# The last layer normalisation of a decoder layer, in pieces of two tiles and with its steps dealt out anew among VectorE, ScalarE and GpSimd

## The chip, the core and the metric

The kernel runs on one core of a Trainium2 chip. Its time is device time in microseconds (us), and the times below are medians of runs of the whole kernel. A profiled execution gives the rows: each names an engine (PE is TensorE's matrix multiply and PEld its weight load, DVE is VectorE, ACT is ScalarE, POOL is GpSimd, SP is SyncE, which here only issues transfers), a line of the kernel, and what was written from what.

## The reference

A decoder layer on x of 2 x 1024 tokens with 256 features, in float32: self attention, cross attention to 77 rows, and a mixture of 8 experts of which each token takes two. Each of the three ends in a residual sum and a layer normalisation. The change is in the third.

```
def _layernorm(x, g, b):
    m = x.mean(-1, keepdims=True)
    v = ((x - m) ** 2).mean(-1, keepdims=True)
    return (x - m) / jnp.sqrt(v + 1e-05) * g + b
...
x = _layernorm(x + _attn(x, x, x, sa_wq, ..., True), ln1_g, ln1_b)
x = _layernorm(x + _attn(x, encoder_output, encoder_output, ca_wq, ..., False), ln2_g, ln2_b)
x = _layernorm(x + _moe(x, router_w, router_b, e_w1, e_b1, e_w2, e_b2), ln3_g, ln3_b)
```

## The kernel before

The 2048 tokens stand in 16 tiles of 128 tokens, one token in a partition: `res` (called residual in the rows) is 128 x 16 x 256 in SBUF. Each engine has one instruction stream, written out by hand, and the streams meet through semaphores (`wait_ge` waits, `then_inc` counts up when the instruction is done). Attention and routing follow a plan, a string of letters that is the same for all engines. Behind it comes a loop over tiles of tokens sorted by expert: TensorE multiplies, ScalarE applies the Gelu (L1123), VectorE adds the bias and the weight (L1345, L1347), and GpSimd adds the finished rows into the table `sums_d` (sums_scratch) in HBM by indirect transfers (L1821).

When the last of these has landed, the third normalisation begins, and nothing else runs from there to the end. It goes over 16 tiles in pieces of `PIECE = 4`:

- SyncE issues the loads of all four pieces from `sums_d` into `res`, 512 KB each (L2085). Then it waits for each finished piece and stores it (L2088), and at last for the stores.
- VectorE takes mean and variance of each tile, `bn_stats` (L1310) and `bn_aggr` (L1312), of which the second waits for the first. After piece n it multiplies the tiles of piece n-1 by the gain row (`gain`, L1352), which waits for ScalarE's result.
- GpSimd makes 1/sqrt(variance + eps) of a piece by a guess and three Newton steps (`normal_scale`, L1792 to L1809): 17 small instructions, in a chain of which each waits for the one ahead. Afterwards it adds the bias row to the tiles of piece n-1 (`shifted`, L1828).
- ScalarE makes x * rstd - mean * rstd of each tile (L1302) as soon as GpSimd has the two columns of that piece.

In GpSimd's stream `normal_scale` of piece n stands ahead of the four adds of piece n-1. `normal_scale` serves the first two normalisations too; lines L1475 and L1478 are theirs on VectorE for half of the tiles, where one `scalar_tensor_tensor` subtracts the mean and multiplies by the gain row, and another scales and adds.

Of the kernel before, what the change touches and what calls it, by code (L numbers as in the profile page):

```python
# [59 lines left out]
PIECE = 4  # L60
# [301 lines left out]
def build(nc, x, ctx_in, par, wts, router_w, w1, b1, w2, b2, out):  # L362
# [3 lines left out]
    with stack:  # L366
# [6 lines left out]
        def sems(name, n):  # L373
            return [sem(f"{name}{i}") for i in range(n)]
# [20 lines left out]
        rstd = sb("rstd", [P, NT])  # L395
        newton = sb("newton", [P, 4, QT])
# [217 lines left out]
        for it in find("proj"):  # L614
# [3 lines left out]
        x_in = sems("x_in", B * NG)  # L618
# [21 lines left out]
        maxima_ok, biased, stats_ok, sdev_ok, scaled = (  # L640
            sem("maxima_split"), sem("out_bias_added"), sem("stats_ok"), sem("sdev_ok"), sem("scaled"))
        scaled_last, sums_stats_ok, tops_ok = sem("sums_scaled"), sem("sums_stats_ok"), sem("tops_ok")
        centred, gained, normal_v, normal_g = sem("centred"), sem("gained"), sem("normal_v"), sem("normal_g")
        chosen, hot_ok, counted, routed = sem("chosen"), sem("hot_ok"), sem("counted"), sem("routed")
        logit_sum, logits_taken = sem("logits_summed"), sem("logits_taken")
        exps_in, exps_ok, diff_ok, second_ok = sem("exps_in"), sem("exps_ok"), sem("diff_ok"), sem("second_exp")
        totals_ok, rows_placed, ej_ok = sem("totals_ok"), sem("rows_placed"), sem("tile_experts_ok")
# [13 lines left out]
        sums_in, stored = sems("sums_in", NT // PIECE), sem("out_stored")  # L661
# [70 lines left out]
        def normal_in(cross, b, t):  # L732

            return (normal_v if b else normal_g, apply_n[cross, b, t])

# [36 lines left out]
        def tensor(pe):  # L772
# [47 lines left out]
            for it in plan:  # L820
# [5 lines left out]
                if it.kind in ("xt", "r_turn"):  # L826
                    if it.kind == "r_turn" or it.cross:
                        e.wait_ge(*normal_in(it.kind == "r_turn", it.b, it.t))
                    else:
                        e.wait_ge(x_in[it.b * NG + it.t // QT], 16)  # L830
# [275 lines left out]
        def scalar(act_e):  # L1106
# [191 lines left out]

            for n in range(NT // PIECE):
                act_e.wait_ge(scaled_last, n + 1)  # L1300
                for t in range(n * PIECE, (n + 1) * PIECE):
                    act_e.activation(res[:, t, :], res[:, t, :], ACT.Identity, scale=rstd[:, t:t + 1],  # L1302
                                     bias=shift[:, t:t + 1]).then_inc(centred, 1)


        def vector(dve):
# [41 lines left out]

            def gain(t, row):
                e.wait_ge(centred, N_APPLY + t + 1)  # L1350
                e.wait_ge(param_in, (NPARAM + 1) * 16)
                dve.tensor_tensor(res[:, t, :], res[:, t, :], param[:, row, :], ALU.mult).then_inc(gained, 1)  # L1352
# [415 lines left out]

            for n in range(NT // PIECE):
                e.wait_ge(sums_in[n], 16)  # L1770
                for t in range(n * PIECE, (n + 1) * PIECE):
                    statistics(t, sums_stats_ok)
                for m in ([n - 1] if n else []) + ([n] if n == NT // PIECE - 1 else []):
                    for t in range(m * PIECE, (m + 1) * PIECE):
                        gain(t, G3)


        def gpsimd(pool):
# [45 lines left out]

            def shifted(t, row):
                e.wait_ge(gained, t + 1)
                e.wait_ge(param_in, (NPARAM + 1) * 16)
                pool.tensor_tensor(res[:, t, :], res[:, t, :], param[:, row, :], ALU.add).then_inc(normal_g, 1)  # L1828
# [129 lines left out]
            for n in range(NT // PIECE + 1):  # L1958
                if n < NT // PIECE:
                    e.wait_ge(sums_stats_ok, (n + 1) * PIECE)  # L1960
                    normal_scale(n * PIECE, scaled_last)
                for t in range((n - 1) * PIECE, n * PIECE) if n else ():
                    shifted(t, B3N)


        def sync(sp):
            e = Waiting(sp)
            for b in range(B):
                for u in range(NG):
                    t0 = b * TB + u * QT  # L1970
                    sp.dma_start(res[:, t0:t0 + QT, :], x[b, u * QG:(u + 1) * QG].rearrange(
                        "(t p) n -> p t n", p=P)).then_inc(x_in[b * NG + u], 16)
# [149 lines left out]
```

## Time and profile before

| | |
|---|---|
| median of 3 runs (825.37 to 833.92) | 826.38 us |
| profiled execution, its own time | 823.76 us |
| its span, first to last instruction | 821.9 us |
| PE, DVE, ACT, POOL busy, share of the span | 87%, 50%, 46%, 34% |
| issue of the first load of the last normalisation (L2085) | at 775.82 us |
| first bn_stats of the last normalisation | at 779.90 us |
| issue of the last store (L2088) | at 815.27 us |

The span starts at 0, so the last three lines are places in it. The first four engines' shares are means over the whole span; the last 46 us have another mix, which the windows and the timeline show. Idle time of an engine that does not set the end costs nothing.

### The profile page before, as it was taken

How to read it: one execution, taken by the hardware profiler on the slowest of the kernel's cores; microseconds unless marked ns; L12 is line 12 of the kernel's file. 1: busy time of each engine (PE TensorE's matmuls, PEld its weight loads, DVE VectorE, ACT ScalarE, POOL GpSimd, SP SyncE). 2: the span in 40 equal slices, each digit the busy share in tenths (PEclk: the TensorE clock that was granted, in tenths of full speed). 3: DMA queues.
4: the chain of work that ended last, by engine and by line, in shares of the span. 5: the costliest groups of instructions: out<-in, count | busy, mean ns of one | idle time of the engine just before them, and what ended most of it. 6: DMA issues, size and time to landing. Idle time of an engine off the chain costs nothing.

```text
span 821.9 us, 14648 instructions
## 1 busy us (share of the span) xinstructions
PE 717.3 (87%) x5227; PEld 491.9 (60%) x5227; DVE 407.2 (50%) x964; ACT 375.0 (46%) x764; POOL 277.4 (34%) x502
## 2 busy tenths in 40 slices
PE   6789999999999999999987699993999999999400
PEld 4434444545555555555535578983999999999300
DVE  5668776757757777655785451662111011111153
ACT  3224555565665766777544444330433333333121
POOL 8140300321352323315622152314133333232276
PEclk9969999999999999999998899996999999999755
DMA  9960430452127013113147639877699999999422
GB/s 288 299 148 1 130 104 4 119 154 80 43 76 205 15 42 117 45 51 91 41 160 272 196 109 271 241 239 261 207 322 328 324 328 324 313 341 274 121 72 77
DMA packets 98528, 140.42 MB, mean 171 GB/s; under 512 B 11647, under 2 KB 85605, under 8 KB 95973
## 3 DMA queue, kind: packets, MB, share of 16 engines
q1 hardware_dynamic: 78453, 110.08, 42.3%
q10 hardware_dynamic: 12896, 19.92, 7.4%
q0 software_dynamic: 7104, 9.45, 5.8%
q8 instruction: 43, 0.70, 0.4%
q14 instruction: 32, 0.26, 0.1%
HBM read 108.55 MB, written 30.88 MB: 170 GB/s over the span
## 4 chain that ended last, share of the span: by engine, by line
PE 51%; DMA 31%; POOL 5%; issue 5%; DVE 2%; ACT 2%; SPq 2%; ACTq 1%; POOLq 0%; DVEq 0%
DMA sums_scratch<-arena,scatter_rows 22%; PE out_acc L946 10%; PE score_pair L923 8%; PE work L893 8%; PE work L867 4%; PE work L810 4%; PE work L816 3%; PE work L970 3%; DMA arena<-parts_scratch 3%; DMA parts_scratch<-arena_more 2%; PE score_pair L926 2%; PE work L954 2%; POOL residual L1828 1%; PE work L896 1%; PE work L879 1%
## 5 line engine op out<-in xcount | busy, mean ns | idle before, releaser
L1420 DVE TENSOR_REDUCE neg_part_max<-work 128x1 f32<-128x512 f32 (+4 forms) x368 | 213.3, 625 | 88.2 <-PE work L893 43.5
L1190 ACT ACTIVATE arena<-score_pair 128x1024 f32<-128x1024 f32 (+2 forms) x224 | 178.7, 839 | 92.6 <-PE score_pair L926 60.7
L893 PE MATMUL work<-arena 96*128 96x77 bf16 (+4 forms) x640 | 122.2, 284 | 14.1 <-DMA arena<-parts_scratch 6.4
L923 PE MATMUL score_pair<-arena 99*128 99x512 bf16 (+2 forms) x448 | 113.0, 335 | 4.3 <-DMA arena<-negmax_scratch 3.0
L1821 POOL DMA_INDIRECT sums_scratch<-arena,scatter_rows x36 | 56.7, 1574 | 177.5 <-DMA sums_scratch<-arena,scatter_rows 127.9
L946 PE MATMUL out_acc<-arena 128*32 128x512 f32 (+4 forms) x896 | 104.5, 517 | 5.6 <-ACT arena L1190 5.0
L816 PE MATMUL score_pair<-arena 128*128 128x256 f32 x432 | 97.5, 379 | 0.0
L893 PEld LDWEIGHTS work<-arena 96*128 96x128 bf16 x640 | 49.5, 100 | 78.8 <-issue 39.7
L1345 DVE TENSOR_TENSOR arena<-score_pair,arena 128x256 f32<-128x256 f32 x27 | 11.5, 424 | 170.6 <-PE score_pair L816 161.1
L810 PE MATMUL work<-arena 128*128 128x128 f32 x720 | 86.2, 278 | 1.0 <-ACT arena L1123 0.5
L816 PEld LDWEIGHTS score_pair<-arena 128*128 128x128 f32 x432 | 80.1, 190 | 9.8
L810 PEld LDWEIGHTS work<-arena 128*128 128x128 f32 x720 | 83.7, 194 | 1.6 <-ACT arena L1123 0.6
L1123 ACT ACTIVATE arena<-work,expert_b_cols 128x128 f32<-128x128 f32 x180 | 51.2, 370 | 66.3 <-issue 36.1
L923 PEld LDWEIGHTS score_pair<-arena 99*128 99x128 bf16 (+1 forms) x448 | 41.7, 101 | 52.8 <-issue 24.1
L810 PE MATMUL score_pair<-arena 128*128 128x128 f32 x432 | 50.5, 275 | 0.0
L926 PE MATMUL score_pair<-identb,mask_qk 128*128 128x128 bf16 x256 | 49.8, 219 | 0.0
L810 PEld LDWEIGHTS score_pair<-arena 128*128 128x128 f32 x432 | 49.4, 192 | 0.1
L896 PE MATMUL work<-mask_qk,identb 128*128 128x128 bf16 x256 | 49.2, 222 | 0.0
L1872 POOL TENSOR_TENSOR arena<-arena,arena_more 128x512 f32<-128x512 f32 (+1 forms) x18 | 19.1, 1063 | 88.8 <-ACT arena L1153 88.8
L1123 ACT ACTIVATE arena<-score_pair,expert_b_cols 128x128 f32<-128x128 f32 x108 | 31.0, 370 | 37.4 <-PE score_pair L810 29.4
L867 PE MATMUL work<-arena_more,arena 128*128 128x512 f32 x96 | 47.4, 624 | 0.1
L946 PEld LDWEIGHTS out_acc<-arena 128*32 128x32 f32 (+1 forms) x896 | 19.5, 108 | 36.5 <-issue 27.9
(238 smaller groups left out, 906.2 us busy)
## 6 DMA issues: line engine op xcount, KB each, us to landing
arena<-in_L_xattn_e_w SPq DMA_DIRECT2D x54, 1024.0 KB, 7.8
arena<-parts_scratch SPq DMA_DIRECT2D x24, 768.0 KB, 6.4
arena<-in_L_xattn_e_w ACTq DMA_DIRECT2D x18, 1024.0 KB, 6.2
parts_scratch<-arena_more SPq DMA_DIRECT2D x24, 384.0 KB, 3.3
parts_scratch<-arena_more SPq DMA_DIRECT2D x24, 256.0 KB, 3.4
parts_scratch<-arena_more SPq DMA_DIRECT2D x24, 128.0 KB, 3.6
residual<-in_x SPq DMA_DIRECT2D x4, 512.0 KB, 8.1
tokens_scratch<-residual SPq DMA_DIRECT2D x2, 1024.0 KB, 6.0
```

Source lines behind the costliest of these rows:

```text
L810: m = pe.matmul(to[:, q * P:(q + 1) * P], w1_ring[j % RING1][:, c, f * P:(f + 1) * P], slot_xT[j % 2][:, c, :], start=(c == 0), stop=(c == ...
L816: m = pe.matmul(to, act[j % 2][:, c, :], w2_ring[j % RING2][:, c, :], start=(c == 0), stop=(c == FC - 1))
L867: m = pe.matmul(bank[:, 0:it.w], weights[:, c, st.hh * P:(st.hh + 1) * P], src, start=(c == 0), stop=(c == KC - 1))
L893: m = pe.matmul(bank[:, j * it.w:(j + 1) * it.w], qa[st.half(it.g)][0:R_S, h, n0:n0 + P], k, start=True, stop=not it.last)
L896: m = pe.matmul(bank[:, (j + 1) * it.w - P:(j + 1) * it.w], identb[:, :], mask_qk[:, :], start=False, stop=True)
L923: m = pe.matmul(st2[pair][0:rows, j, 0:w], k, qa[st.half(it.g)][0:R_M, h, skip:QG], start=True, stop=not diagonal)
L926: m = pe.matmul(st2[pair][:, j, 0:P], mask_qk[:, :], identb[:, :], start=False, stop=True)
L946: m = pe.matmul(o_ps[c * VW:(c + 1) * VW, skip:QG], v, pt[buf][0:rows, j, 0:QG - skip], start=first, stop=last)
L1123: m = act_e.activation(act[j % 2][:, c, :], bank[:, q * P:(q + 1) * P], ACT.Gelu, bias=b1_col[:, bass.ds(ex * FC + c, 1)])
L1190: act_e.activation(pt[buf][0:rows, :, 0:w], st2[pair][0:rows, :, 0:w], ACT.Exp, scale=float(HD) ** -0.5).then_inc(pair_taken[pair], 1)
L1420: dve.tensor_reduce(pm[:, it.at, it.t, it.h0:it.h0 + it.nh], bank[:, 0:it.nh * it.w].rearrange("p (j k) -> p j k", j=it.nh), AX.X, ALU.max ...
L1821: pool.indirect_dma_start(sums_d[0:S] if j < NFIRST else sums_d, bass.IndirectOffsetOnAxis(ap=rows_out[:, j:j + 1], axis=0), slot_y[j % RI ...
```

## The change

Pieces are of two tiles: eight loads and eight stores of 256 KB. VectorE takes the statistics of the two tiles, first both `bn_stats`, then both `bn_aggr`. With the mean it then makes (x - mean) * gain in one `scalar_tensor_tensor` per tile, and a `reciprocal` of the two roots that ScalarE has made meanwhile. ScalarE takes the square root of the variances of piece n, and scales the tiles of piece n-1. GpSimd adds the bias row to each tile and does nothing else. One square root of a constant stands ahead of the loop on ScalarE. The loads' semaphores are shared with those of x at the program's start. The first two normalisations are as they were.

```diff
-PIECE = 4
+PIECE = 2
...
+        root = sb("deviation", [P, NT + 1])
...
@@ scalar @@
-            for n in range(NT // PIECE):
-                act_e.wait_ge(scaled_last, n + 1)
-                for t in range(n * PIECE, (n + 1) * PIECE):
-                    act_e.activation(res[:, t, :], res[:, t, :], ACT.Identity, scale=rstd[:, t:t + 1],
-                                     bias=shift[:, t:t + 1]).then_inc(centred, 1)
+            act_e.activation(root[:, NT:], epsc[:, :], ACT.Sqrt)
+            for n in range(NT // PIECE + 1):
+                if n < NT // PIECE:
+                    tiles = slice(n * PIECE, (n + 1) * PIECE)
+                    act_e.wait_ge(sums_stats_ok, (n + 1) * PIECE)
+                    act_e.activation(root[:, tiles], mv[:, tiles, 1], ACT.Sqrt, bias=epsc[:, :]).then_inc(root_ok, 1)
+                for t in range((n - 1) * PIECE, n * PIECE) if n else ():
+                    act_e.wait_ge(inverted, n)
+                    act_e.activation(res[:, t, :], res[:, t, :], ACT.Identity, scale=rstd[:, t:t + 1]).then_inc(sums_scaled, 1)
@@ vector @@
-            for n in range(NT // PIECE):
-                e.wait_ge(sums_in[n], 16)
-                for t in range(n * PIECE, (n + 1) * PIECE):
-                    statistics(t, sums_stats_ok)
-                for m in ([n - 1] if n else []) + ([n] if n == NT // PIECE - 1 else []):
-                    for t in range(m * PIECE, (m + 1) * PIECE):
-                        gain(t, G3)
+            e.wait_ge(param_in, (NPARAM + 1) * 16)
+            for n in range(NT // PIECE):
+                tiles = range(n * PIECE, (n + 1) * PIECE)
+                e.wait_ge(*sums_in(n))
+                for t in tiles:
+                    own.inc(dve.bn_stats(stat[:, t % 2, :], res[:, t, :]))
+                e.wait_ge(vstep, own.n)
+                for t in tiles:
+                    dve.bn_aggr(mv[:, t, :], stat[:, t % 2, :]).then_inc(sums_stats_ok, 1)
+                e.wait_ge(sums_stats_ok, (n + 1) * PIECE)
+                for t in tiles:
+                    m = dve.scalar_tensor_tensor(res[:, t, :], res[:, t, :], mv[:, t, 0:1], param[:, G3, :],
+                                                 ALU.subtract, ALU.mult)
+                e.wait_ge(root_ok, n + 1)
+
+                dve.reciprocal(rstd[:, n * PIECE:(n + 1) * PIECE], root[:, n * PIECE:(n + 1) * PIECE]).then_inc(inverted, 1)
@@ gpsimd @@
-            for n in range(NT // PIECE + 1):
-                if n < NT // PIECE:
-                    e.wait_ge(sums_stats_ok, (n + 1) * PIECE)
-                    normal_scale(n * PIECE, scaled_last)
-                for t in range((n - 1) * PIECE, n * PIECE) if n else ():
-                    shifted(t, B3N)
+            e.wait_ge(param_in, (NPARAM + 1) * 16)
+            for t in range(NT):
+                e.wait_ge(sums_scaled, t + 1)
+                pool.tensor_tensor(res[:, t, :], res[:, t, :], param[:, B3N, :], ALU.add).then_inc(normal_g, 1)
@@ sync @@
-                sp.dma_start(res[:, n * PIECE:(n + 1) * PIECE, :], rows_of(sums_d, n * PIECE)).then_inc(sums_in[n], 16)
+                sp.dma_start(res[:, n * PIECE:(n + 1) * PIECE, :], rows_of(sums_d, n * PIECE)).then_inc(sums_in(n)[0], 16)
```

The change moves instructions on three engines, all behind the expert loop. VectorE at the end of piece 1 before: the statistics go tile by tile, and the four gains of the piece ahead stand between two pieces.

```order
L1310 BN_STATS stat<-residual 128x6
L1312 BN_AGGR mean_var<-stat 128x2
L1352 TENSOR_TENSOR residual<-residual,param_rows 128x256 x4
L1310 BN_STATS stat<-residual 128x6
L1312 BN_AGGR mean_var<-stat 128x2
```

VectorE after, a whole piece and the start of the next (deviation is `root`, rstd its reciprocal):

```order
L1780 BN_STATS stat<-residual 128x6 x2
L1783 BN_AGGR mean_var<-stat 128x2 x2
L1786 SCALAR_TENSOR_TENSOR residual<-residual,mean_var,param_rows 128x256 x2
L1790 RECIPROCAL rstd<-deviation 128x2
L1780 BN_STATS stat<-residual 128x6 x2
```

The pass over the full tile that VectorE adds is now right behind the statistics of the same piece, and one small instruction closes the piece.

ScalarE before, from the last Gelu of the expert loop to its end:

```order
L1123 ISA
L1123 ACTIVATE arena<-work,expert_b_cols 128x128
L1293 UNCONDITIONAL_BRANCH
L1295 UNCONDITIONAL_BRANCH
L1302 ACTIVATE residual<-residual,minus_mean_scaled,rstd 128x256 x16
L366 UNCONDITIONAL_BRANCH
```

ScalarE after, from the same place on (L1129 is the Gelu, L1306 the root of the constant, L1311 the roots of a piece, L1314 the scaling):

```order
L1129 ACTIVATE arena<-work,expert_b_cols 128x128
L1299 UNCONDITIONAL_BRANCH
L1301 UNCONDITIONAL_BRANCH
L1306 ACT_TABLE_LOAD
L1306 ACTIVATE deviation<-eps 128x1
L1311 ACTIVATE deviation<-mean_var,eps 128x2 x2
L1314 ACTIVATE residual<-residual,rstd 128x256 x2
L1311 ACTIVATE deviation<-mean_var,eps 128x2
L1314 ACTIVATE residual<-residual,rstd 128x256 x2
```

One table load came in, behind the Gelus, and the roots of piece n+1 stand ahead of the scalings of piece n.

GpSimd before, its last instructions, which are the end of the Newton chain of the last piece and eight adds:

```order
L1803 TENSOR_SCALAR newton<-newton 128x4
L1805 TENSOR_TENSOR rstd<-newton,rstd 128x4
L1807 TENSOR_TENSOR newton<-mean_var,rstd 128x4
L1809 TENSOR_SCALAR minus_mean_scaled<-newton 128x4
L1828 TENSOR_TENSOR residual<-residual,param_rows 128x256 x8
L366 UNCONDITIONAL_BRANCH
```

GpSimd after, from the last indirect transfer (L1836) on:

```order
L1964 COMPARE_AND_BRANCH
L1836 DMA sums_scratch<-arena,scatter_rows 2176x256
L1964 UNCONDITIONAL_BRANCH
L1971 TENSOR_TENSOR residual<-residual,param_rows 128x256 x16
L366 UNCONDITIONAL_BRANCH
```

The 17 small instructions of each of the four pieces are gone, and the 16 adds are left.

## Rows read from the trace of the kernel before

**Rows 1.** The chain that ended last, 779.9 to 815.3 us, its shares by line.

```profile
by line: POOL residual L1828 33.0%; issue 14.3%; POOL newton L1803 8.5%; POOL newton L1801 7.7%; POOL newton L1799 7.6%; POOL rstd L1805 7.1%; DVE stat L1310 4.0%; POOL rstd L1795 3.0%; POOL newton L1792 3.0%; POOL newton L1794 2.7%; POOL m
```

**Rows 2.** Timeline of the last normalisation: start, length (us), instruction [idle before].

```profile
775.82 2.03 SPq L2085 DMA_DIRECT2D residual<-sums_scratch  x4
779.90 0.43 DVE L1310 BATCH_NORM_STATS2 stat<-residual 128x6 f32<-128x256 f32 x1 [9.67 <-DMA residual<-sums_scratch]
780.36 0.18 DVE L1312 BATCH_NORM_AGGREGATE mean_var<-stat 128x2 f32<-128x6 f32 x1
780.46 0.39 DVE L1310 BATCH_NORM_STATS2 stat<-residual 128x6 f32<-128x256 f32 x1
...
787.09 2.07 ACT L1302 ACTIVATE residual<-residual,minus_mean_scaled,rstd 128x256 f32<-128x256 f32 x4 [23.53 <-POOL minus_mean_scaled L1809]
787.72 1.90 DVE L1352 TENSOR_TENSOR residual<-residual,param_rows 128x256 f32<-128x256 f32 x4 [3.48 <-ACT residual L1302]
...
792.83 3.13 POOL L1828 TENSOR_TENSOR residual<-residual,param_rows 128x256 f32<-128x256 f32 x4
793.53 3.05 DVE L1352 TENSOR_TENSOR residual<-residual,param_rows 128x256 f32<-128x256 f32 x4 [1.78 <-ACT residual L1302]
...
800.93 3.13 POOL L1828 TENSOR_TENSOR residual<-residual,param_rows 128x256 f32<-128x256 f32 x4
...
815.27 0.37 SPq L2088 DMA_DIRECT2D out<-residual  x1
```

**Rows 3.** Single lines, ns of one instruction as min/median/max, first and last start.

```profile
L1828 POOL TENSOR_TENSOR residual<-residual,param_rows x16: 717/812/907, 792.8 to 814.5; 128x256 f32<-128x256 f32 x16
L1352 DVE TENSOR_TENSOR residual<-residual,param_rows x16: 412/938/986, 787.7 to 812.4; 128x256 f32<-128x256 f32 x16
L1302 ACT ACTIVATE residual<-residual,minus_mean_scaled,rstd x16: 585/586/600, 787.1 to 810.6; 128x256 f32<-128x256 f32 x16
L1475 DVE SCALAR_TENSOR_TENSOR residual<-residual,mean_var,param_rows x16: 474/479/594, 344.1 to 528.4; 128x256 f32<-128x256 f32 x16
L1226 ACT ACTIVATE combine<-weight_tmp x2: 208/208/208, 444.4 to 559.1; 128x8 f32<-128x8 f32 x2
```

**Rows 4.** Transfers from 775 us on: size, median issue to landing; loads' landing by min/median/max.

```profile
residual<-sums_scratch SPq DMA_DIRECT2D x4, 512.0 KB, 5.6
out<-residual SPq DMA_DIRECT2D x4, 512.0 KB, 2.9
DMA to landing us min/median/max: 4.1/5.6/6.9
```

**Rows 5.** Windows from the first load's issue: engines' busy time, last number GB/s.

```profile
775.80:778.80 3.00, 0.00 (x0) 0.00 (x0) 0.00 (x0) 0.00 (x0) 0.00 (x0) 0.50 0.47 129
775.80:779.90 4.10, 0.00 (x0) 0.00 (x0) 0.00 (x1) 0.00 (x0) 0.00 (x0) 0.50 0.63 195
```

**Rows 6.** Timeline of VectorE in the first normalisation.

```profile
344.74 0.49 DVE L1478 SCALAR_TENSOR_TENSOR residual<-residual,rstd,param_rows 128x256 f32<-128x256 f32 x1
345.14 0.48 DVE L1475 SCALAR_TENSOR_TENSOR residual<-residual,mean_var,param_rows 128x256 f32<-128x256 f32 x1
```

**Rows 7.** Timeline at 413 us: statistics on VectorE beside an add on GpSimd.

```profile
413.28 0.73 POOL L1907 TENSOR_TENSOR residual<-residual,param_rows 128x256 f32<-128x256 f32 x1
...
413.58 0.43 DVE L1310 BATCH_NORM_STATS2 stat<-residual 128x6 f32<-128x256 f32 x1
```

**Rows 8.** Groups of VectorE by form: count, busy us and mean ns, idle before.

```profile
L1406 DVE SCALAR_TENSOR_TENSOR arena<-work,bias_columns,arena_more 128x512 f32<-128x512 f32 x8 | 6.0, 750 | 8.9 <-ACT arena_more L1148 8.9
...
L1406 DVE SCALAR_TENSOR_TENSOR arena<-work,bias_columns,arena_more 128x77 f32<-128x77 f32 x2 | 0.6, 299 | 3.3 <-ACT arena_more L1148 3.3
...
L1686 DVE RECIPROCAL prob_recip<-prob_recip 128x8 f32<-128x8 f32 x2 | 0.4, 203 | 0.1
```

**Rows 9.** Timeline of ScalarE at a table load in the routing.

```profile
550.64 1.28 ACT L1220 ACT_TABLE_LOAD   x1
551.93 0.26 ACT L1220 ACTIVATE arena_more<-arena_more 128x64 f32<-128x64 f32 x1
```

More of the change, by code:

```diff
@@ L615, in build @@
             first_of[it.n] = sum(z.st.in_a_hurry for z in find("proj")[:it.n]) + 1
-        x_in = sems("x_in", B * NG)
+        res_in = sems("residual_in", NT // PIECE)
         w_self_in = sems("w_self_in", 4)
@@ L639, in build @@
         vstep, astep, gstep = sem("vector_step"), sem("scalar_step"), sem("gpsimd_step")
[L640 to L644, printed above, removed]
+        maxima_ok, biased, stats_ok, scaled = (
+            sem("maxima_split"), sem("out_bias_added"), sem("stats_ok"), sem("scaled"))
+        sums_scaled, sums_stats_ok, tops_ok = sem("sums_scaled"), sem("sums_stats_ok"), sem("tops_ok")
+        root_ok, inverted = sem("root_ok"), sem("roots_inverted")
+        centred, normal_v, normal_g = sem("centred"), sem("normal_v"), sem("normal_g")
+        hot_ok = sem("hot_ok")
         logit_sum, logits_taken = sem("logits_summed"), sem("logits_taken")
         exps_in, exps_ok, diff_ok, second_ok = sem("exps_in"), sem("exps_ok"), sem("diff_ok"), sem("second_exp")
-        totals_ok, rows_placed, ej_ok = sem("totals_ok"), sem("rows_placed"), sem("tile_experts_ok")
+        rows_placed, ej_ok = sem("rows_placed"), sem("tile_experts_ok")
         rows_ok, kinds_ok, out_rows_ok = sem("rows_ok"), sem("kinds_ok"), sem("out_rows_ok")
@@ L660, in build @@
         y_ok = sem("y_ok")
-        sums_in, stored = sems("sums_in", NT // PIECE), sem("out_stored")
+        stored = sem("out_stored")
         up_banks = work + [st2[1][:, 0, :], st2[1][:, 1, :], o_ps[:, :]]
@@ L734, in normal_in, with sums_in @@
             return (normal_v if b else normal_g, apply_n[cross, b, t])
+        def sums_in(n):
+            return res_in[n], 16 * (2 if n < B * NG else 1)
         def kuse_in(st):
@@ L829, in tensor @@
                     else:
-                        e.wait_ge(x_in[it.b * NG + it.t // QT], 16)
+                        e.wait_ge(res_in[it.b * NG + it.t // QT], 16)
                     e.wait_ge(ident_ok, 1)
@@ L1347, in weighted @@
                 dve.tensor_scalar(y, y, w_slot[:, j:j + 1], None, ALU.mult).then_inc(y_ok, 1)
[L1349 to L1352, printed above, removed]
             dve.memset(ident[:, :], 0.0).then_inc(zeroed, 1)
@@ L1823, in add_up @@
                     compute_op=ALU.add).then_inc(slot_y_out(j)[0], 16)
[L1825 to L1828, printed above, removed]
             e.wait_ge(zeroed, 1)
@@ L1971, in sync @@
                     sp.dma_start(res[:, t0:t0 + QT, :], x[b, u * QG:(u + 1) * QG].rearrange(
-                        "(t p) n -> p t n", p=P)).then_inc(x_in[b * NG + u], 16)
+                        "(t p) n -> p t n", p=P)).then_inc(res_in[b * NG + u], 16)
             for i in range(4):
```

## The prediction

> **What bounds the kernel now.** I read the page's chain first. Most of it is attention and the expert loop, which the change doesn't touch; what matters here is that the last normalisation runs alone, so that every microsecond saved in it is one of the span. It starts with the loads at 775.82 us and ends with the span at 821.9. Its parts: 4.1 us until the first load has landed [rows 2], 35.3 us from the first bn_stats at 779.9 to the end of the last add, and 6.7 us behind that, for the last store (issue at 815.27, 2.9 us to landing [rows 2, 4]) and the program's end, 3.7 us.
>
> For the 35.3 us I read the chain by line [rows 1]. The adds of L1828 and the small instructions of the Newton chain fill nearly all of it, GpSimd's two jobs one after the other. The timeline says how fast it goes: the adds of one piece of four tiles start at 792.83, those of the next at 800.93 [rows 2]. So a piece costs 8.1 us, 3.1 for four adds and the rest for the 17 chained instructions. ScalarE stood idle for 23.5 us ahead of its first scaling [rows 2], VectorE waits for ScalarE. GpSimd is the bound of this stage by a wide margin.
>
> **The change part by part.** I lay a new timetable, piece of two tiles by piece.
>
> Removed from GpSimd: 4 x 17 small instructions. That leaves 16 adds. One alone takes 0.72 us and the next starts 0.68 after it, so its floor is 10.9 us, far below the rest of this sum. The adds only have to keep up.
>
> VectorE, per piece. An instruction that doesn't wait for the one ahead starts 0.08 us before that one's end (aggr at 780.36 for 0.18, the next stats at 780.46 [rows 2]); one that waits starts 0.03 to 0.04 after it (stats 779.90 for 0.43, aggr at 780.36). With 0.39 for bn_stats and 0.18 for bn_aggr: first stats 0.31, second 0.43 with the wait behind it, first aggr 0.10, second 0.22 with the wait. The new full pass has its own row in the first normalisation, same operation, same shape, same kind of scalar: 0.479 us at the median [rows 3], and 0.40 from one start to the next when nothing is waited for (344.74 to 345.14 [rows 6]). Two of them 0.80. The reciprocal is 0.20 us, from a row of 8 columns where here there are 2 [rows 8], 0.12 until the next start. Sum: 0.31 + 0.43 + 0.10 + 0.22 + 0.80 + 0.12 = 1.98 us a piece.
>
> ScalarE, per piece: a small activation at 0.21 [rows 3] and two scalings of 0.59 that start about 0.5 apart (four in 2.07 [rows 2]), 1.15 us of issue in all. That is under VectorE's 1.98. The roots are asked for when the statistics are done and are ready 0.25 later; VectorE wants them 0.8 later, behind its two passes. So the root costs nothing as long as those passes cover it. In ScalarE's queue the root of piece n+1 stands ahead of the scaling of piece n, so the scaling waits for the statistics of the next piece: a lag of about 1 us, paid by nobody until the last piece, where no root stands in front.
>
> The added wait of VectorE is the one on the roots, with the next piece's statistics queued behind it. The added waits of GpSimd queue nothing but adds.
>
> The table load. ScalarE's last Gelu is over 23.5 us before 787.09, at 763.6 [rows 2]; the load and the root of the constant stand right behind it, 12 us ahead of the first load's issue. A load takes 1.28 us, and the next activation starts 1.29 after the load's start [rows 9]. Hidden, and without that cover it would cost 1.3. The build has one such row behind the Gelus, so scaling needs no other table.
>
> SyncE's queue gets eight issues at about 0.5 us each instead of four (2.03 us for four [rows 2]). The eighth load leaves some 2 us later than the fourth did. VectorE wants piece 7 only 14 us after piece 0, so that is hidden. The first piece, half as large, is where I expect a small gain. The 512 KB piece was there at 779.9, when 195 GB/s x 4.1 us = 800 KB had been moved in all, since pieces behind it share the engines. At the same share 262 KB are there when 400 KB have moved, which the trace had about 778.8 (129 x 3.0 = 387 [rows 5]). Bounds 778.8 and 779.9; I take 779.0.
>
> The last store is half as large. 512 KB took 2.9 us to land; loads streamed 512 KB in about 1.4 us at full rate (800 - 387 KB in 1.1 us), so half of that less gives 2.2. Bounds 1.9 and 2.9.
>
> Now the sum. First statistics 779.0; those of piece 0 done 1.0 later (0.31 + 0.43 + 0.10 + 0.18): 780.0. Those of piece 7 come 7 x 1.98 = 13.9 later: 793.9. Behind them on ScalarE: root 0.24, scalings of piece 6 until 1.24, those of piece 7 ending at 1.8 and 2.3. GpSimd adds piece 6 from 0.9 to 2.2 and piece 7 from 2.2 to 3.6: 797.5. Store 2.2, program's end 3.7: span 803.4, against 821.9. That is 18.5 us less, 805.3 for the profiled execution. It stands 2.6 us under the median of 826.38; taken off the median the 18.5 give **807.9**, and I say 808.0.
>
> **Contention.** What the sum leaves out is that VectorE's passes with two inputs in SBUF and GpSimd's adds hold each other up. L1352 takes 0.41 alone and 0.94 beside an add, and the adds go from 0.72 to 0.91 [rows 3]; four gains take 1.90 us alone and 3.05 beside adds, which then take 3.13 for four [rows 2]. Statistics are free of it: bn_stats wholly inside an add took 0.43 as ever [rows 7]. In my timetable adds of piece n-1 run from 0.9 to 2.2 us behind piece n's statistics, and VectorE's passes from 0.0 to 0.85 and from 2.0 on. So the adds lie mostly beside statistics and touch a pass by 0.1 or 0.2 us. This is luck of phase. I leave it at nothing and put the bad phase among the rivals.
>
> A rule speaks against the new pass. The row shows 0.479 us for `scalar_tensor_tensor` on two float32 tiles in SBUF against 0.41 for `tensor_tensor` on such tiles [rows 3]. The Trainium skill, Vector Engine (DVE) Microarchitecture Reference, section 7 (Points that are easy to get wrong), says that a `scalar_tensor_tensor` with two SBUF sources other than bf16 runs at half throughput. By that rule the passes would be longer and the forecast 4.1 us later, which is the second rival; the trace of before disagrees, in 16 instructions of that very form.
>
> **Rivals.**
>
> Lockstep. Passes and adds meet every time. The phase isn't fixed: a pass that is held up ends later, which pulls the next piece's adds along. Then each of the two passes costs what a gain cost between adds, 0.88 from start to start ((3.05 - 0.41) / 3 [rows 2, 3]), and a piece 1.98 + 2 x 0.48 = 2.94 us. 7 x 2.94 = 20.6 in place of 13.9: 6.7 more, 814.6. For it: the rows of L1352. Against it: GpSimd is idle for a third of each piece, and the timetable puts that third beside the passes. The Trainium skill, GPSIMD Engine Reference, section 1 (Specifications), says that its SBUF interfaces are shared with VectorE, with contention from VectorE instructions that have two SBUF inputs; the rows above agree.
>
> The pass at half rate. An element costs 1.04 ns in this operation, (750 - 299) / (512 - 77) [rows 8]; twice that for 256 elements adds 0.27 us a pass, 0.53 a piece, 3.7 over seven pieces, and 0.4 at the end, where the last reciprocal would now come later than ScalarE's queue allows: 812.1. Against it: the 0.479 above.
>
> The change doesn't do what it says: ScalarE changes table for every root and back. 2 x 1.29 more in a piece [rows 9] makes ScalarE the bound, 2.6 + 1.15 + 0.1 = 3.85 a piece; 780.0 + 8 x 3.85 + 0.7 + 2.2 + 3.7 = 817.4, 4.5 less than before: 821.9, within 1%. Against it: the build has one load.
>
> Slower. Each of the eight loads pays its whole time from issue to landing behind the one ahead, as if they went one by one: 5.6 us each [rows 4], last at 775.8 + 44.8 = 820.6, then 1.0 + 3.6 + 2.2 + 3.7 for the rest: span 831.1, 835.6 on the median. It decides from 4.45 us a load. Against it: the four loads before were all in within 8.4 us, though each took 4.1 to 6.9.
>
> **How the numbers follow.** The timetable as laid, 0.75. Lockstep 0.12, half rate 0.04, table changes 0.03, one-by-one loads 0.02; 0.04 for what I don't see. The main case alone has the bounds 778.8 and 1.9 below (0.5 less) and 779.9, 2.9 and a held-up first pass of 0.2 a piece above (0.9 + 0.7 + 1.4 = 3.0 more), so 807.4 to 811. Medians of three wander by about a microsecond (825.37 and 826.38 among the three of before), and my step times could be off by a tenth a piece to either side, which is why the range begins at 805.5. Above it goes to 812.5, which takes in half rate and the milder half of lockstep. What a measurement can tell from no change is about 1%, 8 us. Faster by more than that: all but tables, loads and part of the unseen, 0.93. Within 1%: 0.05. Slower: 0.02.
>
> **What would show it.** In the trace of the changed kernel: a table load near 764 us and none later; the first bn_stats at about 779.0; starts of the first bn_stats of neighbouring pieces 2.0 apart, with VectorE busy throughout and idle for no root; the new pass at 0.48, and at 0.6 or more where an add crosses it; adds 0.68 apart in pairs with gaps between pairs; eight stores 2 us apart; the last add ending near 797.5. A distance of 2.5 or 2.9 speaks for a rival. I would be wrong if an instruction stream stalls where I laid none: ScalarE late with a root, since that sits in one queue with the scalings, or a pass caught in every piece.

## The result and the profile after

The changed kernel took 806.52 us at the median of 4 runs (801.18 to 807.22), the kernel before 827.04 (825.37 to 833.92): a ratio of 0.9745, with a 95% interval of 0.9709 to 0.978. The forecast was 808.0, from 805.5 to 812.5. The same kernel run again later, beside the kernel before, gave 805.98 against 824.4, a ratio of 0.9791 (0.9763 to 0.9819).

The profiled execution took 807.22 us with a span of 805.4. Its first load went out at 777.63 us, 1.8 later than in the profile of before; that head wanders by a few microseconds from one execution to the next (777.63 and 774.12 in the two profiles of the changed kernel), and no instruction was moved in it. So I compare the last stretch, from the issue of the first load to the end of the span: 46.1 us before, 27.8 after, 18.3 less. The forecast for it was 18.5. The second profile of the changed kernel gives 27.8 again.

The chain of the stretch from 777 us on, its shares by line (lines of the changed kernel: L1786 is VectorE's pass, L1780 and L1783 the statistics, L1971 the adds):

```profile
by line: DVE residual L1786 22.0%; DVE stat L1780 18.6%; DMA residual<-sums_scratch 9.5%; POOL residual L1971 7.2%; DVE mean_var L1783 7.2%; issue 3.2%; POOLq L366 2.3%; DVE rstd L1790 1.8%; ACT residual L1314 1.4%; ACT deviation L1311 1.0%
```

In [rows 1] nearly all was GpSimd's. Now VectorE has the chain, and GpSimd only its end. The timeline, for the first load, pieces 0 to 2, and the last piece (start, length, instruction, idle before):

```profile
777.63 3.96 SPq L2093 DMA_DIRECT2D residual<-sums_scratch  x8
780.40 0.75 DVE L1780 BATCH_NORM_STATS2 stat<-residual 128x6 f32<-128x256 f32 x2 [8.49 <-DMA residual<-sums_scratch]
781.18 0.25 DVE L1783 BATCH_NORM_AGGREGATE mean_var<-stat 128x2 f32<-128x6 f32 x2
781.47 0.30 ACT L1311 ACTIVATE deviation<-mean_var,eps 128x2 f32<-128x2 f32 x1 [13.55 <-DVE mean_var L1783]
781.47 0.88 DVE L1786 SCALAR_TENSOR_TENSOR residual<-residual,mean_var,param_rows 128x256 f32<-128x256 f32 x2
782.27 0.16 DVE L1790 RECIPROCAL rstd<-deviation 128x2 f32<-128x2 f32 x1
782.34 0.73 DVE L1780 BATCH_NORM_STATS2 stat<-residual 128x6 f32<-128x256 f32 x2
...
784.24 1.40 POOL L1971 TENSOR_TENSOR residual<-residual,param_rows 128x256 f32<-128x256 f32 x2 [9.43 <-ACT residual L1314]
784.26 0.73 DVE L1780 BATCH_NORM_STATS2 stat<-residual 128x6 f32<-128x256 f32 x2
785.03 0.25 DVE L1783 BATCH_NORM_AGGREGATE mean_var<-stat 128x2 f32<-128x6 f32 x2
...
785.32 1.00 DVE L1786 SCALAR_TENSOR_TENSOR residual<-residual,mean_var,param_rows 128x256 f32<-128x256 f32 x2
...
785.67 13.42 SPq L2096 DMA_DIRECT2D out<-residual  x8
786.09 1.49 POOL L1971 TENSOR_TENSOR residual<-residual,param_rows 128x256 f32<-128x256 f32 x2 [0.45 <-ACT residual L1314]
...
792.16 0.73 DVE L1780 BATCH_NORM_STATS2 stat<-residual 128x6 f32<-128x256 f32 x2
...
794.11 0.73 DVE L1780 BATCH_NORM_STATS2 stat<-residual 128x6 f32<-128x256 f32 x2
...
795.15 0.30 ACT L1311 ACTIVATE deviation<-mean_var,eps 128x2 f32<-128x2 f32 x1 [0.86 <-DVE mean_var L1783]
795.15 0.90 DVE L1786 SCALAR_TENSOR_TENSOR residual<-residual,mean_var,param_rows 128x256 f32<-128x256 f32 x2
795.36 1.72 ACT L1314 ACTIVATE residual<-residual,rstd 128x256 f32<-128x256 f32 x4
795.92 2.77 POOL L1971 TENSOR_TENSOR residual<-residual,param_rows 128x256 f32<-128x256 f32 x4 [0.55 <-ACT residual L1314]
```

Read against [rows 2]: pieces of two tiles now start 1.92 to 1.95 us apart (780.40, 782.34, 784.26, and near the end 792.16, 794.11), where four tiles took 8.1. Nothing is left between VectorE's steps but gaps of 0.02 to 0.04 us. The last add ends at 795.92 + 2.77 = 798.69, and the span 6.7 us later, as before. The single lines, against [rows 3] (ns as min/median/max):

```profile
L1786 DVE SCALAR_TENSOR_TENSOR residual<-residual,mean_var,param_rows x16: 472/482/607, 781.5 to 795.6; 128x256 f32<-128x256 f32 x16
...
L1971 POOL TENSOR_TENSOR residual<-residual,param_rows x16: 717/722/811, 784.2 to 798.0; 128x256 f32<-128x256 f32 x16
...
L1314 ACT ACTIVATE residual<-residual,rstd x16: 491/492/507, 783.6 to 796.6; 128x256 f32<-128x256 f32 x16
```

The new pass takes what its row of the first normalisation said. The adds are back at 0.72 but for one, and the scaling is 0.09 us shorter without its bias column. The transfers, against [rows 4]:

```profile
residual<-sums_scratch SPq DMA_DIRECT2D x8, 256.0 KB, 4.4
out<-residual SPq DMA_DIRECT2D x8, 256.0 KB, 2.1
```

### The profile page after: what moved, and what is told of

Its sections match the earlier page's. It is cut to its first block, busy times and chain, and to the rows that moved or that the text cites. A ratio compares the mean times of both kernels' runs of the same rounds, so it can differ in the third digit from the quotient of the medians.

```text
span 805.4 us, 14606 instructions
## 1 busy us (share of the span) xinstructions
PE 720.3 (89%) x5227; PEld 496.8 (62%) x5227; DVE 404.0 (50%) x972; ACT 376.5 (47%) x774; POOL 260.7 (32%) x434
## 4 chain that ended last, share of the span: by engine, by line
PE 54%; DMA 29%; DVE 5%; issue 5%; ACT 2%; POOL 2%; ACTq 1%; SPq 1%; POOLq 0%; DVEq 0%
DMA sums_scratch<-arena,scatter_rows 22%; PE out_acc L952 10%; PE score_pair L929 8%; PE work L899 8%; PE work L873 5%; PE work L816 4%; DMA arena<-parts_scratch 4%; PE work L822 3%; PE work L976 3%; PE work L885 2%; DVE neg_part_max L1426 2%; PE score_pair L932 2%; PE work L960 2%; PE work L902 2%; DMA parts_scratch<-arena_more 1%
## 5 line engine op out<-in xcount | busy, mean ns | idle before, releaser
L1836 POOL DMA_INDIRECT sums_scratch<-arena,scatter_rows x36 | 56.7, 1574 | 179.4 <-DMA sums_scratch<-arena,scatter_rows 127.4
L816 PE MATMUL work<-arena 128*128 128x128 f32 x720 | 89.8, 285 | 0.7 <-ACT arena L1129 0.5
L816 PEld LDWEIGHTS work<-arena 128*128 128x128 f32 x720 | 87.3, 201 | 1.4 <-ACT arena L1129 0.6
L1129 ACT ACTIVATE arena<-work,expert_b_cols 128x128 f32<-128x128 f32 x180 | 51.1, 369 | 69.2 <-issue 37.7
L1129 ACT ACTIVATE arena<-score_pair,expert_b_cols 128x128 f32<-128x128 f32 x108 | 30.9, 369 | 37.4 <-PE score_pair L816 29.4
```

The source lines that it names most:

```text
L816: m = pe.matmul(to[:, q * P:(q + 1) * P], w1_ring[j % RING1][:, c, f * P:(f + 1) * P], slot_xT[j % 2][:, c, :], start=(c == 0), stop=(c == ...
L1129: m = act_e.activation(act[j % 2][:, c, :], bank[:, q * P:(q + 1) * P], ACT.Gelu, bias=b1_col[:, bass.ds(ex * FC + c, 1)])
L1836: pool.indirect_dma_start(sums_d[0:S] if j < NFIRST else sums_d, bass.IndirectOffsetOnAxis(ap=rows_out[:, j:j + 1], axis=0), slot_y[j % RI ...
```

## The experiments

All are read by the last stretch, from the first load's issue to the end of the span, and by the distance between pieces in it. The head varies more than most of these effects, while the stretch repeats within 0.1 us: 27.8 in both profiles of the changed kernel, 31.2 and 31.1 in the two forms with pieces of four. Whole times stand where a kernel was timed in several runs.

**Small pieces with the old dealing out.** The kernel before with pieces of two, with the loads' semaphores shared as in the changed kernel:

```diff
-PIECE = 4
+PIECE = 2
...
-            def normal_scale(t0, done):
+            def normal_scale(t0, done, n=QT):
...
-                    normal_scale(n * PIECE, scaled_last)
+                    normal_scale(n * PIECE, scaled_last, PIECE)
```

Expected: 

> The kernel before with pieces of two tiles and nothing else: the Newton chain stays on GpSimd, now on two columns and eight times instead of four. Theory A (the gain of the change comes from taking the chain off GpSimd): a chain costs about 4.9 us whatever its width, since it is 17 small instructions that wait for each other, so 8 x 4.9 + 16 adds in 12.4 us = 52 us in place of 33; the first load lands 1.3 us sooner and the first statistics are done 1.1 us sooner, so the span is about 16.5 us longer than before, some 843 us. Theory B (the gain comes from the smaller pieces, which overlap better): shorter than before by a good part of the 18 us.

Measured: 840.0 us against 823.44 of before, ratio 1.0187 (1.0148 to 1.0227), and 61.9 us for the last stretch. GpSimd's timeline, from the first instruction of a chain to that of the next:

```profile
797.72 1.41 POOL L1831 TENSOR_TENSOR residual<-residual,param_rows 128x256 f32<-128x256 f32 x2
799.21 0.27 POOL L1795 TENSOR_SCALAR newton<-mean_var 128x2 f32<-128x2 f32 x1
804.01 1.41 POOL L1831 TENSOR_TENSOR residual<-residual,param_rows 128x256 f32<-128x256 f32 x2
```

A chain on two columns takes 4.8 us, from 799.21 to 804.01, and one on four columns 5.0 (8.1 less 3.1 for the adds [rows 2]). Theory A holds. Small pieces alone, without the new dealing out, cost 15.8 us.

**The new dealing out with pieces of four.** The changed kernel with

```diff
-PIECE = 2
+PIECE = 4
...
-        stat = sb("stat", [P, 2, 6])
+        stat = sb("stat", [P, 4, 6])
...
-                    own.inc(dve.bn_stats(stat[:, t % 2, :], res[:, t, :]))
+                    own.inc(dve.bn_stats(stat[:, t % 4, :], res[:, t, :]))
...
-                    dve.bn_aggr(mv[:, t, :], stat[:, t % 2, :]).then_inc(sums_stats_ok, 1)
+                    dve.bn_aggr(mv[:, t, :], stat[:, t % 4, :]).then_inc(sums_stats_ok, 1)
```

Expected: 

> The changed kernel with pieces of four tiles. Theory A (the dealing out of the steps is what pays): from the first load's issue to the end about 2.3 us more than the 27.8 us of the changed kernel, 1.3 of it because 512 KB land 1.3 us later than 256 KB and 1.0 because the last piece's four adds trail behind VectorE. Theory B (piece size is at least half of the gain): 9 us more or worse, so that this stretch takes 37 us or more.

In this first form the helper of the first two normalisations wrote its statistics to one of four slots and read one of two, so their variances, and with them the routing, weren't the reference's. It took 809.67 us and 31.2 us for the last stretch. The second form has `t % 4` in that helper's reading too.

Expected: 

> The changed kernel with pieces of four tiles, the statistics of the first two normalisations read from the slots they were written to. (The first kernel of this kind read two of four from the wrong slot there; its last stretch took 31.2 us from first load to end, where 30.1 had been expected by theory A.) Theory A, the dealing out of the steps pays: 31.2 again, three to four us over the changed kernel's 27.8, of which 1.3 is the later landing of a 512 KB load. Theory B, piece size is at least half of the gain: 37 us or more.

Measured: 808.59 us against 824.4, ratio 0.9798 (0.9771 to 0.9826), last stretch 31.1 us. The timeline of VectorE's passes in pieces 0, 1 and 2, with the adds of piece 1:

```profile
786.07 1.67 DVE L1786 SCALAR_TENSOR_TENSOR residual<-residual,mean_var,param_rows 128x256 f32<-128x256 f32 x4
...
789.57 2.14 DVE L1786 SCALAR_TENSOR_TENSOR residual<-residual,mean_var,param_rows 128x256 f32<-128x256 f32 x4
...
793.54 2.64 DVE L1786 SCALAR_TENSOR_TENSOR residual<-residual,mean_var,param_rows 128x256 f32<-128x256 f32 x4
...
794.31 3.13 POOL L1971 TENSOR_TENSOR residual<-residual,param_rows 128x256 f32<-128x256 f32 x4 [0.66 <-ACT residual L1314]
```

So of the 18.3 us, 15.0 are there with pieces of four (46.1 to 31.1), and 3.3 come with pieces of two. Theory A holds, with 1.0 us more than I had first reckoned. The rows say where that is: four passes take 1.67 us alone, 2.64 beside adds. With pieces of four the two meet, and the distance between pieces grows from 3.5 over 4.0 to 4.5. Of the 3.3 us, 1.2 are the later first statistics (4.0 us behind the load's issue where it's 2.8 with pieces of two).

**Steps of one tile.** Loads and stores stay at two tiles; everything between goes tile by tile:

```diff
+STEP = 1
...
-            for n in range(NT // PIECE):
-                tiles = range(n * PIECE, (n + 1) * PIECE)
-                e.wait_ge(*sums_in(n))
+            for n in range(NT // STEP):
+                tiles = range(n * STEP, (n + 1) * STEP)
+                e.wait_ge(*sums_in(n * STEP // PIECE))
```

Expected: 

> The changed kernel with loads and stores of two tiles as now, but statistics, root, pass, reciprocal and scaling one tile at a time. Each tile then pays the two waits on VectorE alone: about 1.17 us a tile in place of 0.98, 3.1 us more over the 16, less about 1.3 us because the last tile's scaling and add trail less. Theory A (VectorE's issue and waits set the pace): about 29.6 us from first load to end, 1.8 more than now. Theory B (the trailing of the last piece matters more than the waits): the same or less than 27.8.

Measured: 30.5 us, 2.7 more than the changed kernel. VectorE at two neighbouring tiles, with an add beside the second pass:

```profile
790.26 0.49 DVE L1787 SCALAR_TENSOR_TENSOR residual<-residual,mean_var,param_rows 128x256 f32<-128x256 f32 x1
...
791.03 0.72 POOL L1972 TENSOR_TENSOR residual<-residual,param_rows 128x256 f32<-128x256 f32 x1 [0.57 <-ACT residual L1315]
...
791.40 0.64 DVE L1787 SCALAR_TENSOR_TENSOR residual<-residual,mean_var,param_rows 128x256 f32<-128x256 f32 x1
```

Theory A, and the 0.9 us beyond it has the same source as above: every other pass lies in an add for 0.35 us (791.40 to 791.75) and takes 0.64.

**Scaling ahead of the root.** ScalarE's loop in the other order, nothing else:

```diff
+                for t in range((n - 1) * PIECE, n * PIECE) if n else ():
+                    act_e.wait_ge(inverted, n)
+                    act_e.activation(res[:, t, :], res[:, t, :], ACT.Identity, scale=rstd[:, t:t + 1]).then_inc(sums_scaled, 1)
                 if n < NT // PIECE:
...
-                for t in range((n - 1) * PIECE, n * PIECE) if n else ():
-                    act_e.wait_ge(inverted, n)
-                    act_e.activation(res[:, t, :], res[:, t, :], ACT.Identity, scale=rstd[:, t:t + 1]).then_inc(sums_scaled, 1)
```

Expected: 

> The changed kernel with ScalarE's two steps of a turn in the other order: first the scalings of piece n-1, then the root of piece n. The adds then come 0.7 us behind the reciprocal and fall on VectorE's next two passes. Theory A (passes with two SBUF inputs and GpSimd's adds exclude each other, and the changed kernel avoids it by its phase): the distance between pieces goes from 1.95 to about 2.6 us, passes that meet an add take 0.6 to 1.0 us, and the stretch from first load to end is 3 to 4 us longer than 27.8. Theory B (the phase doesn't matter): distance stays at 1.95, and the last adds come 0.6 us sooner, 27.2.

Measured: 31.6 us, 3.8 more. Its timeline over one piece:

```profile
782.19 1.59 POOL L1971 TENSOR_TENSOR residual<-residual,param_rows 128x256 f32<-128x256 f32 x2 [0.97 <-ACT residual L1310]
...
782.54 1.52 DVE L1786 SCALAR_TENSOR_TENSOR residual<-residual,mean_var,param_rows 128x256 f32<-128x256 f32 x2
...
784.75 1.59 POOL L1971 TENSOR_TENSOR residual<-residual,param_rows 128x256 f32<-128x256 f32 x2 [0.97 <-ACT residual L1310]
...
785.10 1.52 DVE L1786 SCALAR_TENSOR_TENSOR residual<-residual,mean_var,param_rows 128x256 f32<-128x256 f32 x2
```

From piece 1 on both passes of every piece are caught: 1.52 us for two in place of 0.90, and a distance of 2.56 (782.54 to 785.10) in place of 1.95. This is the lockstep rival, made on purpose. The order of two small loops on ScalarE decides over it, because it sets when the adds fall. The 0.6 us that the other order was expected to save at the end don't show: the last add ends 3.6 us behind the last statistics, where it is 3.5 in the changed kernel, since the last two passes are caught too.

**No pass on VectorE.** Centring and gain are left out:

```diff
-                for t in tiles:
-                    m = dve.scalar_tensor_tensor(res[:, t, :], res[:, t, :], mv[:, t, 0:1], param[:, G3, :],
-                                                 ALU.subtract, ALU.mult)
```

Expected: 

> The changed kernel without VectorE's pass over the full tile: centring and gain are left out of the output. Theory A (VectorE sets the pace): the distance between pieces falls from 1.95 to about 1.45 us, now with a wait for the root in it, and the stretch from first load to end falls by 3.5 us to about 24.3. Theory B (ScalarE or GpSimd sets the pace): distance stays at 1.9 or so, no change.

Measured: 25.3 us, 2.5 less. The reciprocals of pieces 0 and 1, and the statistics of piece 2:

```profile
781.85 0.17 DVE L1787 RECIPROCAL rstd<-deviation 128x2 f32<-128x2 f32 x1 [0.44 <-ACT deviation L1311]
...
783.38 0.17 DVE L1787 RECIPROCAL rstd<-deviation 128x2 f32<-128x2 f32 x1 [0.44 <-ACT deviation L1311]
...
784.09 0.75 DVE L1780 BATCH_NORM_STATS2 stat<-residual 128x6 f32<-128x256 f32 x2 [0.54 <-DMA residual<-sums_scratch]
```

The distance falls to 1.53 us, with the wait for the root (0.44) open that the passes used to cover. So VectorE set the pace of the changed kernel; here the pace is that of VectorE and the root in turn. The forecast missed 1 us: half of it is the 0.54 us wait for the third load, which at this pace comes too late, the other half 0.08 a piece.

**No early table load.**

```diff
-            act_e.activation(root[:, NT:], epsc[:, :], ACT.Sqrt)
```

Expected: 

> The changed kernel without the root of the constant ahead of the loop, so that ScalarE's table load stands in front of the first real root. Theory A (the early root hides the load in idle time, and VectorE has 0.5 us of slack on the first root): VectorE's first reciprocal comes 0.8 us later, and with it everything behind, 28.6 us from first load to end in place of 27.8. Theory B (a change of table costs a pipeline drain as well, 2.7 us in all): 2.2 us later. Theory C (the load is fetched ahead of the wait): no change.

Measured: 27.7 us, no change, theory C. ScalarE's timeline:

```profile
764.91 1.28 ACT L1310 ACT_TABLE_LOAD   x1 [1.17 <-ACTq L1284]
780.28 0.29 ACT L1310 ACTIVATE deviation<-mean_var,eps 128x2 f32<-128x2 f32 x1 [14.08 <-DVE mean_var L1782]
```

The load stands in front of the first real root now, and still ran 14 us ahead of it. The wait holds up the root and not the load. The early root of the constant does nothing.

**Bias adds of the last tiles on VectorE.** In the profile of after one thing stood out: the last store landed at 800.9 us, 2.2 after the last add, where before it was 3.0 behind it, and yet the end kept its 6.7 us from the last add. SyncE's waits at the end of the changed kernel (us in total, times, longest; L366 is the program's end, where all engines meet):

```profile
SPq L366 <- PEq L366: 4.3, 1, 4.3
...
SPq L366 <- DMA out<-residual: 1.8, 1, 1.8
```

SyncE has its store home and then waits 4.3 us more for the program's end; before it was 3.6. The row names PE's sequencer, which had no work since the expert loop; I took GpSimd to be what it waits for. The edit, with k = 2, 4 and 6:

```diff
-            for t in range(NT):
+            for t in range(NT - k):
                 e.wait_ge(sums_scaled, t + 1)
                 pool.tensor_tensor(res[:, t, :], res[:, t, :], param[:, B3N, :], ALU.add).then_inc(normal_g, 1)
...
+            for t in range(NT - k, NT):
+                e.wait_ge(sums_scaled, t + 1)
+                dve.tensor_tensor(res[:, t, :], res[:, t, :], param[:, B3N, :], ALU.add).then_inc(normal_v, 1)
...
-                sp.wait_ge(normal_g, N_APPLY + (n + 1) * PIECE)
+                if (n + 1) * PIECE <= NT - k:
+                    sp.wait_ge(normal_g, N_APPLY + (n + 1) * PIECE)
+                else:
+                    sp.wait_ge(normal_v, N_APPLY + (n + 1) * PIECE - (NT - k))
```

Two adds. Expected: 

> The changed kernel with the bias adds of the last two tiles on VectorE, which is free by then. In both traces the program ends 6.7 us after GpSimd's last add, although the last store landed 0.8 us sooner behind it in the changed kernel. Theory A (the end is set by GpSimd's own closing, 6.5 us from its last add): GpSimd's last add ends 1.4 us earlier, and so does the program, 26.4 us from first load to end. Theory B (the end is set by the last store's landing): the last add ends near 797.5 in the changed kernel's time in place of 798.7, 1.2 us less. The two agree here; the next kernel parts them.

Measured: 26.4 us, 1.4 less, as both theories said.

Four adds. Expected: 

> The changed kernel with the bias adds of the last four tiles on VectorE. Theory A (GpSimd's own closing sets the end): GpSimd's last add ends 3.3 us earlier than in the changed kernel, at 795.4 on its clock, and the program ends 3.3 us earlier, 24.5 us from first load to end, unless the store's landing comes to bind. Theory B (the last store sets the end): the last store goes out when it does with two adds on VectorE, and the program ends only 1.2 us earlier, 26.6.

Measured: 24.3 us, 3.4 less; 804.06 us against 823.08, ratio 0.9771 (0.9739 to 0.9803). Theory A. GpSimd's last adds and VectorE's four in this kernel, whose span is 801.7:

```profile
793.64 1.41 POOL L1974 TENSOR_TENSOR residual<-residual,param_rows 128x256 f32<-128x256 f32 x2 [0.54 <-ACT residual L1314]
...
795.72 1.48 DVE L1793 TENSOR_TENSOR residual<-residual,param_rows 128x256 f32<-128x256 f32 x4
```

GpSimd's last add ends at 795.05, and 801.7 is again 6.7 behind it, although VectorE worked on until 797.2.

Six adds. Expected: 

> The changed kernel with the bias adds of the last six tiles on VectorE. In all eight kernels of this study so far the program ended 6.71 us after GpSimd's last add, whatever the store did. Theory A: that goes on until the last store binds. GpSimd's last add ends about 15.7 us after the first load's issue, 22.4 with its closing; VectorE's last add ends 0.6 us later than with four, 20.4, and the store lands at 22.6, so the end is at 22.6 to 23.5, one to two us below the 24.3 with four adds. Theory B (the store and something of 2.3 us behind its landing set the end already with four adds): the end comes 0.6 us later than with four, 24.9.

Measured: 23.3 us for the last stretch; 802.3 us against 824.4, ratio 0.9741 (0.9714 to 0.9768). SyncE's waits of this kernel:

```profile
SPq L366 <- DMA out<-residual: 2.0, 1, 2.0
SPq L366 <- PEq L366: 0.2, 1, 0.2
```

The 4.3 us of waiting behind the store are gone. Now the store binds: six adds run in 2.08 us on VectorE, the last store goes out at 20.5 us of the stretch and lands 2.4 later, and the program ends 0.4 us after that. GpSimd's last add is 7.4 us from the end here, the only kernel in which it isn't 6.7.

The traces hold a record that bears this out and that the views don't print: GpSimd has one at L366, named DRAIN. In the changed kernel it ends at 805.16, and the span at 805.40; with four adds on VectorE it ends at 801.51, and the span at 801.75. With six it ends at 800.51, ahead of the store's landing at 801.09, and no longer counts.

**No bias adds at all.** The bias is missing from the output:

```diff
             for t in range(NT):
-                e.wait_ge(sums_scaled, t + 1)
-                pool.tensor_tensor(res[:, t, :], res[:, t, :], param[:, B3N, :], ALU.add).then_inc(normal_g, 1)
...
-                sp.wait_ge(normal_g, N_APPLY + (n + 1) * PIECE)
+                sp.wait_ge(sums_scaled, (n + 1) * PIECE)
```

Expected: 

> The changed kernel with all 16 bias adds left out: the bias is missing from the output, and SyncE stores a piece when ScalarE has scaled it. GpSimd's closing can start behind its last indirect transfer, far ahead. This shows the end that the store alone allows. VectorE's passes meet no add, so the distance between pieces is 1.95 throughout; the last scaling ends at 19.4 us from the first load's issue, the store lands at 21.6. If the store's landing needs the same 2.3 us behind it as in the kernel with four adds on VectorE, the end is at 23.9; if that was still GpSimd's closing, at 22 or so.

Measured: 21.8 us (777.10 to 798.9). So six adds on VectorE leave 1.5 us that the adds still cost, and the 2.3 us behind the store in the kernel with four adds were GpSimd's. Here the program ends 0.4 us behind the last store's landing, and GpSimd's DRAIN is over at 780.57. Without adds the pieces are 1.92 us apart throughout, so in the changed kernel, at 1.95, passes and adds cost each other 0.2 us in all.

**The changed kernel once more.** Expected: 

> The changed kernel itself once more, unaltered, on the same chip as the kernel with six adds on VectorE, so that the two can be compared through the same runs of the kernel before: about 0.977 of before, the last stretch 27.8 us, against about 0.971 and 23 for the one with six adds.

Measured: 27.8 us for the last stretch (774.12 to 801.9), 805.98 us. With six adds on VectorE the same chip gave 802.3. That is 3.7 us less by the medians and 4.5 by the last stretch. The intervals of the two ratios, 0.9763 to 0.9819 and 0.9714 to 0.9768, overlap at their edges, so the times alone don't settle it. I take the version with six adds as the best of the study, on the strength of the trace.

## Why the prediction was right

The forecast stands on a timetable of the last stretch, and the trace lets each step be held against it. The mechanism was right. That the stretch came out within 0.2 us (27.6 forecast, 27.8 measured) is in part luck: the end was 0.8 us longer than laid, and the first load and the pieces shorter by about 0.6.

**GpSimd as the bound, and the chain as its cost.** Right, and shown twice: pieces of two without the new dealing out made the kernel 15.8 us slower in that stretch, the new dealing out with pieces of four gave 15.0 of the 18.3 us. That the four chains were the larger part is reckoned from their 5.0 us each and not shown by itself: no run takes the chain off GpSimd and leaves centring, gain and their waits as they were.

**First statistics 3.2 us after the first load's issue.** It was 2.8 (777.63 to 780.40). I had scaled the time of the 512 KB piece by how much had been moved in all, 400 KB for half a piece. By 780.40 some 470 KB had been moved (168 GB/s over 2.8 us), so the share of the first piece was smaller than taken, and the transfers together were quicker.

**1.98 us a piece on VectorE.** It was 1.92 to 1.95, and 2.06 once. The parts were off by a little: the steps up to the passes took 1.04 to 1.07 us instead of 1.06, the passes 0.80 to 0.84 instead of 0.80, and the reciprocal, at 0.15 instead of 0.20, let the next piece start after 0.08 and not 0.12. The root took 0.30, not 0.21, on an engine that had room for it. Taking VectorE's pass away lowered the distance, so it was the bound as laid.

**3.6 us from the last statistics to the last add.** It was 3.5 (795.15 to 798.69).

**Contention left at nothing.** Right for the reason given, with one exception, piece 2 in the timeline above, where the phase isn't yet that of the others: the adds of piece 0 (784.24 to 785.64) reach 0.3 us into the first pass, and those of piece 1 begin at 786.09, 0.2 us before the second ends. The two passes take 1.00 us and the two adds 1.49. I called it luck, and the order reversed on ScalarE showed it to be: 3.8 us. The rival's own price was 6.7. It was too high because one of the two passes crosses an add only in part, 0.66 and not 0.94, so that a piece took 2.56 and not 2.94.

**The store of 2.2 us and 3.7 us of program's end.** This step failed, though it moved the sum by only 0.8 us. The store did land in 2.1. But the 3.7 us were no fixed end behind the store. They were what was left of GpSimd's 6.7 us from its last add to the end of the span, and that doesn't shrink with a smaller store: it was 6.7 too with two and with four adds on VectorE, while the store's landing moved from 2.2 to 4.4 us behind GpSimd's last add. The row to distrust was SyncE's wait at the end of the program, which I hadn't read.

**Half rate for the pass**, the rule of the Trainium skill (Vector Engine (DVE) Microarchitecture Reference, section 7): 0.482 us at the median in 16 instructions, as the trace of before had it, where half rate was reckoned to add 0.27. The measurement decides: the rule doesn't hold for this form.

**Table changes for every root**: one load, at 766.4 us. **Loads one by one**: the eight loads took 4.4 us each at the median, but overlapped, and VectorE waited once, for the first.

By the profiles the gain is 18.3 us; the medians say 20.5 in the first comparison and 18.4 in the second. The 2 us beyond the stretch lie in the head, where the kernels are alike, or in the few runs; no run here says which.

## What to carry to other kernels

A chain of small instructions that wait for each other cost its count and not its width here (17 of them 4.8 us on two columns, 5.0 on four); on the engine that also has the wide work, it is the first thing to move, and making pieces smaller ahead of that makes it worse. Before a timetable is trusted, lay the two-input passes of VectorE over GpSimd's over time: whether they meet was worth 3.8 us of 28 here, and turned on the order of two waits on a third engine. And look at which engine the program's end waits for: the last four adds take 2.8 us on GpSimd, and moving them to VectorE shortened the kernel's last stretch by 3.4, because the wait of 0.55 us ahead of them went too.

## What the runs showed of the hardware

The program's end came 6.7 us after GpSimd's last add in twelve of the thirteen profiles that have adds there, whether the last store landed 2.2 or 4.4 us behind that add. When GpSimd was done early enough, the end came 0.4 us after the last store's landing. GpSimd's DRAIN record ended 6.47 us after its last add in all thirteen, and with no adds 6.5 us after its last transfer instruction. What GpSimd does in that time no record shows.

A table load on ScalarE didn't wait for the activation behind it: it ran 14 us ahead, 1.2 us behind the last Gelu. The Trainium skill, ScalarE: Activation LUTs, section What ACT_TABLE_LOAD costs, counts a drain of 1.38 us besides the 1.28 us of the load; in the trace of before the load at 550.64 starts 0.02 us after the end of the activation ahead of it, and the next activation 1.29 us after the load's start [rows 9]. The trace has no room for the drain there.

A scaling on ScalarE took 0.49 us with a column for the scale alone, 0.59 with a column for the bias too [rows 3]. Statistics and aggregation on VectorE ran at full speed beside adds on GpSimd (0.73 and 0.25 us for two, as without them: 784.26, 785.03 against 782.34, 781.18); the pass with two tiles from SBUF did not, at 0.61 to 0.98 us against 0.48.
